# Moving the layer-norm statistics of a later chunk between the scans of the current one, in an RWKV + FFN layer on eight cores

## What is computed

```python
xn = _layernorm(x)
k = xn @ Wk.T ; r = xn @ Wr.T ; v = r
# wkv_scan, per channel, over time (numerically stable form left out):
#   y_t = (a + e^(u+k_t) v_t) / (b + e^(u+k_t))
#   a = e^w a + e^k_t v_t ;  b = e^w b + e^k_t ,   w = -exp(time_decay), u = time_first
attn = (sigmoid(r) * wkv_scan(w, u, k, v)) @ Wo.T
ffn  = (silu(xn @ wg.T) * (xn @ wu.T)) @ wd.T     # wg, wu, wd = int / 127, hidden 3072
out  = x + attn + ffn
```

## Time and profile before

| | us |
|---|---|
| two timed runs | 2108.95 and 2266.35, median 2187.65 |
| the profiled execution, device time | 2098.2 |
| its span on the slowest core (core 7) | 2096.5 |
| spans of the eight cores | 2079.7 to 2096.5 |
| granted clock of the cores, mean, share of full speed | 0.869 to 0.877 |

### The profile page before, as it was taken

One profiled execution on the slowest core, in us unless ns is written; L12 is line 12 of the kernel. 1 busy time (PEld: TensorE's weight loads), 2 busy tenths in 40 slices (PEclk: granted clock), 3 DMA queues, 4 the chain that ended last, 5 costly groups with the idle time before them and its releaser, 6 DMA issues.

```text
span 2096.5 us, 24763 instructions; the slowest of 8 cores (2079.7 to 2096.5 us)
## 1 busy us (share of the span) xinstructions
PE 1540.9 (73%) x8192; PEld 804.3 (38%) x8192; DVE 626.1 (30%) x1094; ACT 467.9 (22%) x803; POOL 121.7 (6%) x112
## 2 busy tenths in 40 slices
PE   2645446544554521998998998998998998998995
PEld 2434345433543411443433433433433433433432
DVE  0465576566755800211211211211201201201201
ACT  3234444444444431210110110200100100200100
POOL 1001111111121110000000000000000000000000
PEclk9877667766776655999999999999999999999998
DMA  6213344434443567646746746747747747747741
GB/s 99 73 41 81 81 106 116 101 81 103 118 102 81 102 132 188 153 126 181 181 124 187 176 125 199 162 123 204 164 119 211 160 117 211 160 117 213 158 118 64
DMA packets 573610, 280.58 MB, mean 134 GB/s; under 512 B 477232, under 2 KB 526384, under 8 KB 573488
## 3 DMA queue, kind: packets, MB, share of 16 engines
q1 hardware_dynamic: 557744, 237.05, 44.4%
q0 software_dynamic: 15744, 41.95, 10.4%
HBM read 251.70 MB, written 52.43 MB: 145 GB/s over the span
## 4 chain that ended last, share of the span: by engine, by line
PE 71%; DMA 11%; ACT 7%; issue 5%; DVE 5%; POOL 0%; SPq 0%; ACTq 0%; DVEq 0%; POOLq 0%
PE psA L638 16%; PE psB L649 16%; PE psRb L679 9%; PE psK L444 6%; PE psR L444 6%; DMA pp_in<-wu 4%; PE psB L679 4%; PE psA L679 4%; PE psRb L691 3%; ACT S L525 3%; DMA pp_in<-wd 3%; ACT S L521 2%; DVE res L700 1%; PE psB L691 1%; PE psA L691 1%
## 5 line engine op out<-in xcount | busy, mean ns | idle before, releaser
L638 PE MATMUL psA<-xnc,wgu 128*128 128x512 bf16 x1536 | 375.5, 389 | 55.1 <-DVE res L700 30.0
L649 PE MATMUL psB<-xnc,wgu 128*128 128x512 bf16 x1536 | 366.7, 382 | 0.0
L657 ACT ACTIVATE sil<-psA,cst 128x512 f32<-128x512 f32 x192 | 131.9, 687 | 1035.6 <-PE psA L638 1035.6
L662 DVE SCALAR_TENSOR_TENSOR h_sb<-sil,cst,psB 128x512 bf16<-128x512 f32 x192 | 143.5, 748 | 594.4 <-PE psB L649 523.2
L638 PEld LDWEIGHTS psA<-xnc,wgu 128*128 128x128 bf16 x1536 | 152.3, 100 | 245.6 <-issue 71.9
L679 PE MATMUL psRb<-wdt,h_sb 128*128 128x512 bf16 x768 | 196.5, 377 | 36.3 <-DVE h_sb L662 8.9
L649 PEld LDWEIGHTS psB<-xnc,wgu 128*128 128x128 bf16 x1536 | 151.7, 99 | 186.0 <-issue 8.2
L419 PE MATMUL psT<-identsb,xn_tok 128*128 128x128 bf16 x256 | 29.8, 308 | 203.7 <-DVE xn_tok L409 203.7
L700 DVE TENSOR_TENSOR res<-psRb,x 128x512 f32<-128x512 f32 x32 | 22.1, 692 | 525.8 <-PE psB L691 522.9
L444 PE MATMUL psK<-xn_fm,wkT 128*128 128x256 bf16 x1024 | 152.5, 298 | 3.1 <-ACT xn_fm L426 3.1
L444 PE MATMUL psR<-xn_fm,wrT 128*128 128x256 bf16 x1024 | 146.3, 290 | 5.3 <-DVE S L464 5.1
(11 more groups left out here) (58 smaller groups left out, 1059.3 us busy)
## 6 DMA issues: line engine op xcount, KB each, us to landing
wgu<-wgu_s SPq DMA_DIRECT2D x192, 512.0 KB, 4.4
wdt<-wdT_s SPq DMA_DIRECT2D x192, 256.0 KB, 2.7
x_tok<-x SPq DMA_DIRECT2D x16, 1024.0 KB, 6.3
x<-x SPq DMA_DIRECT2D x8, 2048.0 KB, 14.6
out<-res POOLq DMA_DIRECT2D x8, 2048.0 KB, 8.1
wgu_s<-pp_stage SPq DMA_DIRECT2D x48, 256.0 KB, 3.4
xn_s<-xn_fm SPq DMA_DIRECT2D x16, 512.0 KB, 5.8
outp_s<-outb SPq DMA_DIRECT2D x16, 512.0 KB, 5.3
```

What stands on the lines that cost most here:

```text
L638: last = e.matmul(psA[pab][:], wgu_t[wsl][:, (iu * CC + cc) * P:(iu * CC + cc + 1) * P], xnc[sl][:, cc * TT2:(cc + 1) * TT2], start=(cc == ...
L649: last = e.matmul(psB[pab][:], wgu_t[wsl][:, (iu * CC + cc) * P:(iu * CC + cc + 1) * P], xnc[sl][:, cc * TT2:(cc + 1) * TT2], start=(cc == ...
L657: lambda e, pab=pab: e.activation(out=sil_b[pab][:], in_=psA[pab][:], func=AF.Silu, scale=cst[:, 3:4]),
L662: lambda e, hc=hc, pab=pab: e.scalar_tensor_tensor(out=h_sb[:, hc * TT2:(hc + 1) * TT2], in0=sil_b[pab][:], scalar=cst[:, 4:5], in1=psB[pa ...
```

## The change

`stage_a` is cut in three: `stage_a_stats` (statistics, Ln and Exp), `stage_a_apply` (normalization) and `stage_a_post` (transposes, copies, store). `stage_c` is cut in two, scans for a range of blocks, and the elementwise half. The loop calls them in another order: statistics and normalization of chunk ch+2 stand behind the first ten scans of chunk ch, and its transposes, copies and store behind B(ch+1) and ahead of D(ch). Statistics of both tiles now stand ahead of both normalizations. The load of x keeps its place at the head of the iteration. No instruction, buffer or shape is changed.

```diff
-            def stage_a(ch):
-                t0 = ch * TT1
+            def stage_a_stats(ch):
                 sl = ch % 2
                 for ts in range(TS1):
...
                           reads=[r_lnv[sl], r_cst], writes=[r_rstd[sl]])
+
+            def stage_a_apply(ch):
+                sl = ch % 2
+                for ts in range(TS1):
                     bd.op("vector",
                           lambda e, sl=sl, ts=ts: e.tensor_scalar(
...
                           reads=[r_x_tok[0], r_mv[sl], r_rstd[sl]], writes=[r_xn_tok[0]])
+
+            def stage_a_post(ch):
+                t0 = ch * TT1
+                sl = ch % 2
                 for ts in range(TS1):
                     def tr(e, sl=sl, ts=ts):
...
-            def stage_c(ch):
+            def stage_c_scans(ch, lo, hi):
                 sl = ch % 2
                 ol = 1 - sl
-                for cc in range(CC):
+                for cc in range(lo, hi):
                     b0 = cc * (TT1 + 1)
...
+
+            def stage_c_stt(ch):
+                sl = ch % 2
                 for cc in range(CC):
                     sli = slice(cc * TT1, (cc + 1) * TT1)
...
             stage_a_dma(0)
-            stage_a(0)
+            stage_a_stats(0)
+            stage_a_apply(0)
+            stage_a_post(0)
             stage_b(0)
             stage_a_dma(1)
-            stage_a(1)
+            stage_a_stats(1)
+            stage_a_apply(1)
+            stage_a_post(1)
             for ch in range(NC1):
                 if ch + 2 < NC1:
                     stage_a_dma(ch + 2)
-                stage_c(ch)
+                stage_c_scans(ch, 0, 5)
+                if ch + 2 < NC1:
+                    stage_a_stats(ch + 2)
+                    stage_a_apply(ch + 2)
+                stage_c_scans(ch, 5, CC)
+                stage_c_stt(ch)
                 if ch > 0:
                     stage_e(ch - 1)
                 if ch + 1 < NC1:
                     stage_b(ch + 1)
+                if ch + 2 < NC1:
+                    stage_a_post(ch + 2)
                 stage_d(ch)
-                if ch + 2 < NC1:
-                    stage_a(ch + 2)
                 n_units = (len(pp_units) * (ch + 1)) // NC1
```

## The result

The changed kernel takes 2238.7 us (median of 12 runs) against 2108.5 (median of 10 of the kernel before, on the same chip). The ratio is 1.0625, 95% interval 1.0598 to 1.0653: some 132 us slower. The predicted time was 2252 us, in a range of 2205 to 2310.

A forecast was written before the change was run, and what follows sets the result against it. A chain of waits, no full engine, bounds the kernel; after the change VectorE waits for x, issued behind four weight stores. +158 (iterations 3 to 13), +0.6 and -4.7 give +154 on 2098.2: 2252 us, range 2205 to 2310.

The forecast's parts named there:

- its landing: SP's queue: an iteration's first weight store lands in the median 3.4 us, bounded by 2.6 and 8.4.
- statistics start: VectorE: statistics wait for the load of x until 25 us after the iteration's start, idle for 18.5 us.
- A on VectorE: VectorE: statistics and normalization of both tiles take 5.3 us, the first normalization lying under the second wait for rstd.
- iterations 0 to 2: Loop start, no weight stores ahead of x: 128.3 us together against 127.7, so +0.6 us.
- the part ahead of the loop: Before the loop: the first two chunks' statistics each join two serial rounds, -4.7 us together.
- the rest behind S of iteration 14: From the start of iteration 14's scans to the kernel's end: left alone by the change, no time won or lost.
- the main term: Iterations 3 to 13: 56.3 us each, against 461.5 us in all before, +158 us.
- The compute taken out from between: Between issue of x and its reader: 22 us less compute, weighed by a skill rule the sum doesn't need.
- the shortest landings: Lower end of the range: landings of 2.6 us (store) and 5.6 us (x) take off 15 us.
- ScalarE's queue is the gate: Rival: x early enough, Ln and Exp wait behind the last weight copy; 46.3 us an iteration, 2142 us, chance 0.03.
- The clock rival: Rival: the stall is there but TensorE keeps 2.4 GHz, 8.73 us instead of 11.5; 2221 us, chance 0.07.
- the contention rival: Rival: an iteration's first weight store still takes 8.4 us to land, +5 us x 11; 2307 us, chance 0.10.

The follow-up runs named there:

- e1: Changed kernel, with the load of x for chunk ch+3 issued on SP right behind the normalization of ch+2, ahead of the weight stores: 2126.7 us.
- e2: Changed kernel, with statistics and normalization moved back behind stage_c's elementwise half, the load of x left in place: 2104.5 us.
- e8: Kernel before, with only statistics and normalization moved between the scans; transposes, copies and store of x stay behind stage_d: 2256.9 us.
- e5: Changed kernel, with a separate resource per token tile for mean, ln and rstd: 2223.5 us.
- e3: Kernel before, all of stage_a still behind stage_b, but both tiles' statistics joined and stage_a ahead of stage_d: 2039.1 us.
- e7: Changed kernel, statistics and normalization between second and third product of stage_b, load of x issued behind them, rstd resources by tile: 1935.7 us.
- e6: Changed kernel, with statistics and normalization behind stage_c's elementwise half and the load of x issued right behind the normalization: 2044.0 us.
- e4: Changed kernel, with 380 unused identity transposes on TensorE ahead of stage_b's third pair in iterations 3 to 13: 2229.5 us.

## Why the prediction was right

Its steps against the changed kernel's iteration 6 (S = 383.32), offsets from S:

| step | predicted | measured |
|---|---|---|
| ScalarE through with D, first weight copy | 9.1 | 8.6 |
| first weight store | 10.2 | 9.7 |
| its landing | 3.4 | 2.6 |
| landing to issue of x | 5.0 | 5.1 |
| issue of x | 18.6 | 17.35 |
| statistics start | 25.0 | 22.9 |
| A on VectorE | 5.3 | 6.4 |
| six scans, C's second half, E | 14.45 | 14.5 |
| first product to next iteration | 11.5 | 11.2 |
| iteration | 56.3 | 55.0 |

The mechanism is the predicted one, and e1, e2 and e8 show it from three sides. Take the load out from behind the stores, and the wait for x goes; move the reader, and the load doesn't follow; make the reader's move alone, and the whole loss is there.

Two terms were mis-sized, in opposite directions. The statistics start 2.1 us earlier than forecast. Of that, 0.5 is ScalarE, 0.8 the first store and 0.8 the load of x, which landed after 5.5 us in this iteration (median 6.3 before). I had taken the median of all 48 stores for the first one of an iteration, though I had argued that nothing runs beside it any more; then the minimum of the earlier trace rows, 2.6, is the row to take. Landings of the changed kernel's 48 wgu stores, minimum, median, maximum:

```profile
DMA to landing us min/median/max: 2.6/2.8/3.6
```

And A on VectorE was 1.1 us too small: I had let the first normalization slip under the wait for the second tile's rstd. `Build.op` waits by resource, and both tiles' rstd are one resource, whose last writer is now the second Exp. The code told that; I had read only the durations. e5 shows it.

The smaller terms: iterations 0 to 2 came out at +1.6 (predicted +0.6), the part ahead of the loop at -3.5 (-4.7), and the rest behind S of iteration 14 was 3.5 us shorter, which I had put at nothing. That last one needs no cause in the change: in the changed kernel's own trace this stretch takes 1409.1 us on core 0 and 1415.7 on core 2, and the slowest cores of all ten traces have it between 1412.5 and 1421.1. With +145.0 for the main term instead of +158 the sum is 139.6 in the spans. The medians give 130, the ratio 132.

Two slips of the prediction's arithmetic change nothing in it. The compute taken out from between is 23.2 us by its own offsets (29.6 - 6.4), not 22. And the shortest landings are worth 1.5 us in each of 11 iterations, that is 16.5 us and not 15; with 16.5 the lower bound comes out at the stated 2205.

Of the rivals, "ScalarE's queue is the gate" did not decide the changed kernel, but is real: it is what e1 ran into, at 44.7 us an iteration where I had put 46.3 for it. The wait of 16.9 us an iteration for x decides against it in the changed kernel: an issue is short (0.47 us), but its place in the queue cost 17 us. By the Trainium skill (DMA: Bandwidth & Descriptors, Issuing engines are not separate DMA queues), starting DMAs from several engines saves only the time that starting one takes on the sequencer, which is usually small relative to the DMA. For the issue alone the trace agrees: 0.47 us beside 5.5 us to landing. What cost 17 us here is the wait of the issues ahead of it, and e1 shows that with another place in the same queue; no run gives the load to another engine's queue. The clock rival (8.73 kept) falls by the granted clock of 0.50 at 372.5, and the contention rival by the landings above: the longest is 3.6 us, not 8.4.

What the prediction had not seen: what the other half of the change is worth by itself. e3 is 69 us faster than the kernel before. In its trace 48 us of that are won in iterations 3 to 13 (413.5 against 461.5), where VectorE waits 62 us less for rstd and 9.5 more in the products, and 12 us in iterations 0 to 2 (115.95 against 127.67).

## What to carry to other kernels

Before moving a reader forward in its engine's queue, find where its load is issued in the queue of the issuing engine, and what that queue waits for ahead of it; a load's place in the code is not its place in time. Compare the landing, not the length of the transfer, with the new place of the reader, and then ask the same of every other queue the moved work passes: here ScalarE's, behind SP's, was the next gate. Work that has slack did best where its engine waits anyway (e7, 31.0 us an iteration), better than where its engine is busy and the load is there in time (e6, 37.5).

## What the runs showed of the hardware that was not expected

The landing of a 256 KB weight store went with its neighbours: 7.2 us beside two weight loads and the xn store, 3.8 us with the xn store 0.9 us ahead (3.6 to 4.9 over the iterations of e8), 2.6 us alone.

TensorE was still at a granted clock of 1.00 after 1.9 us of standing still in one iteration of e4; after 2.8 us in the next one, the following 5.3 us averaged 0.68. In the changed kernel it stood still for 9.1 us, worked off one group, stood still for 14.7 us, and the following 5.1 us were at 0.50. The length of the pause alone didn't decide it: in iteration 6 of e6 TensorE went on at 1.00 after 2.85 us.
